# Attention outputs normalised through memory: stores, column reciprocals, a spread over rows and a GpSimd product in place of TensorE turns and VectorE divisions

## What is computed

```python
q = _split_heads(Q @ W_Q.T)
k = _split_heads(K @ W_K.T)
v = _split_heads(V @ W_V.T)
scores = jnp.einsum('bhqd,bhkd->bhqk', q, k) / jnp.sqrt(jnp.float32(DK))
scores = jnp.where(mask == 0, -jnp.inf, scores)
weights = jax.nn.softmax(scores, axis=-1)
attn = jnp.einsum('bhqk,bhkd->bhqd', weights, v)
attn = attn.transpose(0, 2, 1, 3).reshape(Q.shape[0], Q.shape[1], D)
return attn @ W_O.T
```

## Time and profile before

| | us |
|---|---|
| median of 3 runs | 1264.85 |
| lowest and highest run | 1264.16, 1265.81 |
| the profiled execution, device time | 1271.13 |
| span of its records | 1269.4 |
| PE busy | 1122.1 (88%) |
| DVE busy | 838.7 (66%) |
| ACT busy | 644.6 (51%) |
| POOL busy | 211.9 (17%) |
| granted PE clock, mean | 0.945 |

### The profile page before, as it was taken

How to read it: one execution, slowest core, us unless ns; L and a number is a source line. 1 busy time by engine, 2 the same in 40 slices (tenths; PEclk the granted TensorE clock), 3 DMA queues, 4 the chain that set the end, 5 groups by cost and what they waited for, 6 DMA issues and landing times. The chain is left out here.

```text
span 1269.4 us, 17696 instructions
## 1 busy us (share of the span) xinstructions
PE 1122.1 (88%) x5578; PEld 540.3 (43%) x5578; DVE 838.7 (66%) x2112; ACT 644.6 (51%) x1341; POOL 211.9 (17%) x273
## 2 busy tenths in 40 slices
PE   7889999999897999999859999996979999998480
PEld 4433343434453233333355666664523333335350
DVE  5788777776477899898752222224779888867622
ACT  3346666666543676767613333332427767674240
POOL 3310000000143000010212222212410010102244
PEclk9979999999999899999958999998979999999695
DMA  8943221220059334432471130102963323201054
GB/s 256 325 145 113 84 51 51 84 51 1 1 195 278 102 92 114 112 101 77 142 298 34 61 127 28 32 8 99 313 217 88 94 62 87 59 19 67 26 157 141
DMA packets 102868, 139.40 MB, mean 110 GB/s; under 512 B 11189, under 2 KB 84793, under 8 KB 101369
## 3 DMA queue, kind: packets, MB, share of 16 engines
q1 hardware_dynamic: 98696, 128.04, 33.2%
q0 software_dynamic: 4080, 10.23, 2.9%
HBM read 86.30 MB, written 52.17 MB: 109 GB/s over the span
## 5 line engine op out<-in xcount | busy, mean ns | idle before, releaser
L888 ACT ACTIVATE r<-ps 128x512 f32<-128x512 f32 x768 | 428.0, 600 | 209.5 <-PE ps L974 121.5
L377 DVE TENSOR_REDUCE m<-ps 128x1 f32<-128x512 f32 x512 | 320.6, 683 | 33.9 <-PE ps L961 33.9
L974 PE MATMUL ps<-r 99*128 99x512 bf16 x768 | 293.4, 387 | 6.4 <-ACT r L888 5.8
L961 PE MATMUL ps<-r 96*128 96x512 bf16 x720 | 282.2, 393 | 14.4 <-DVE m L377 7.0
L988 PE MATMUL ps<-r 128*32 128x512 f32 x1536 | 204.9, 605 | 5.6 <-ACT r L888 3.3
L373 DVE CUSTOM_DVE_ANT_0 r<-ps,r 128x512 bf16<-128x512 f32 x256 | 170.2, 690 | 53.2 <-PE ps L961 52.5
L974 PEld LDWEIGHTS ps<-r 99*128 99x128 bf16 x768 | 74.3, 98 | 213.8 <-ACT r L888 157.9
L961 PEld LDWEIGHTS ps<-r 96*128 96x128 bf16 x720 | 71.1, 99 | 103.1 <-DVE m L377 30.7
L864 POOL COPY r<-r 128x256 f32<-128x256 f32 x48 | 19.1, 401 | 524.5 <-PE ps L988 524.5
L978 PE MATMUL ps<-r,identb 128*128 128x512 bf16 x256 | 98.2, 384 | 0.0
L1661 DVE COPY r<-ps 128x512 f32<-128x512 f32 x46 | 31.8, 692 | 92.0 <-PE ps L1708 92.0
(11 more groups left out here) (152 smaller groups left out, 1197.7 us busy)
## 6 DMA issues: line engine op xcount, KB each, us to landing
r<-q_parts SPq DMA_DIRECT2D x48, 384.0 KB, 4.5
r<-k_parts SPq DMA_DIRECT2D x48, 384.0 KB, 5.4
k_parts<-r SPq DMA_DIRECT2D x24, 384.0 KB, 3.2
q_parts<-r SPq DMA_DIRECT2D x24, 384.0 KB, 3.2
r<-in_w SPq DMA_DIRECT2D x16, 512.0 KB, 3.7
r<-in_w SPq DMA_DIRECT2D x8, 1024.0 KB, 14.9
k_parts<-r SPq DMA_DIRECT2D x24, 256.0 KB, 3.2
q_parts<-r SPq DMA_DIRECT2D x24, 256.0 KB, 3.1
```

The lines of the kernel that those rows point to most:

```text
L377: ins = dve.tensor_reduce(out, mem.ps[:, bank, :], AX.X, ALU.max)
L888: act.activation(mem.probs[:, u // HG, u % HG, :], ps[:, ST + (UNITS * g + u) % DEEP, :], ACT.Exp, scale=SCALE).then_inc(a.p_exp.sem, 1)
L961: pe.matmul(ps[:, led_bank(n), :], mem.qst[g][0:ROWS, h, t * P:(t + 1) * P], mem.kst[g][0:ROWS, h, :], start=True, stop=True).then_inc(a.s ...
L974: ins = pe.matmul(out, mem.kst[g][0:KROWS, h, kt * P:(kt + 1) * P], mem.qst[g][0:KROWS, h, :], start=True, stop=not a.masked)
```

## The change

Groups 0 to 13 of each stage are no longer turned by PE and divided by DVE. ACT copies the products to `mem.ot` with a bias column (`guard`, 1e-30 on the four rows of sums, 0 elsewhere), and SP stores them to memory (`products`). Two groups are a chunk, 128 rows of outputs. SP loads a chunk's 8 rows of sums as 128 partitions of 32 columns (`sums`) and its outputs as 128x512 (`oTu`), once for every second group, at g = 2 for the batch's first chunk and at g = 0 of the next batch for its second. DVE takes the reciprocal of 128x32 at u = 12, SP stores it, and loads it back with every row repeated 16 times into `mem.oT`; POOL multiplies `oTu` by it in place. Groups 14 and 15 of a stage are turned and divided as before, and one `turn_out` is left at the stage's end. The tiles of the output projection move from (2, 3), (2, 4), (3, 3), (3, 4) to (2, 2), (2, 3), (2, 5), (2, 6). The store of the residual sum in sa0 stays at g = 3. The four shift semaphores become one. The diff, cut to its core:

```diff
...
+        self.sums = sb("sums", [P, C, S // DK])
+        self.recip = sb("recip", [P, C, S // DK])
+        self.guard = sb("guard", [P, 1])
...
         self.ot = take(self.r2, S, [S])
-        self.o = take(self.r2, T * D, [T, D])
+        self.oTu = take(self.r2, C * S, [C, S])
+        self.o = self.oTu[:, C - 1, :].rearrange("p (t d) -> p t d", t=T)
         self.oT = take(self.r2, C * S, [C, S])
...
 KEY_TILES = 2
 MASK_ROUNDS = T // KEY_TILES
 NEXT_STAGE = ((3, 5), (3, 14))
-HALF_TURN = (3, 13)
-LAST_TURN, LAST_OUT = (5, 2), (3, 4)
+LAST_TURN, LAST_OUT = 2, (3, 4)
+RECIP_STEP = 12
+TURNED = NG // C
+TURNED_FROM = B * NG - TURNED
 LATE = 2
 AHEAD = 3
 M_STEP, TURN_STEP = 8, 12
-OUT_TURNS = (3, 5)
-OUT_TILES = ((2, 3), (2, 4), (3, 3), (3, 4))
+OUT_TILES = ((2, 2), (2, 3), (2, 5), (2, 6))
...
+
+    def out_store(G):
+        sp.wait_ge(a.ot_sb.sem, a.ot_sb.at(G, 1))
+        sp.dma_start(a.dram["ot"][G], mem.ot).then_inc(a.sent.sem, 16)
+
+    def out_load(b, c):
+
+        G = NG * b + TURNED * c
+        sp.wait_ge(a.sent.sem, a.sent.at(G + TURNED))
+        if C * b + c:
+            sp.wait_ge(a.oT_sb.sem, C * b + c)
+        heads = a.dram["ot"][G:G + TURNED].rearrange("g (h r) n -> (g h) r n", h=HG)
+        sp.dma_start(mem.sums[:, c, :], heads[:, DK, :].rearrange("g (k n) -> g k n", k=DK))\
+          .then_inc(a.chunk_in.sem, 16)
+        sp.dma_start(mem.oTu[:, c, :], heads[:, 0:DK, :]).then_inc(a.chunk_in.sem, 16)
+
+    def recip_store(b, c):
+
+        sp.wait_ge(a.recip.sem, C * b + c + 1)
+        sp.dma_start(a.dram["recip"][b, c], mem.recip[:, c, :]).then_inc(a.recip_out.sem, 16)
+
+    def recip_spread(b, c):
+
+        sp.wait_ge(a.recip_out.sem, 16 * (C * b + c + 1))
+        if b:
+            sp.wait_ge(a.op_ps.sem, a.op_ps.at(b))
+        rows = a.dram["recip"][b, c].rearrange("(h k) n -> h (k n)", k=DK)
+        sp.dma_start(mem.oT[:, c, :], rows.unsqueeze(1).to_broadcast([P // DK, DK, S]))\
+          .then_inc(a.spread.sem, 16)
...
-            if a.self_block and g == OUT_TILES[-1][0] and not first:
+            if G >= 1 and G - 1 < TURNED_FROM:
+                out_store(G - 1)
+            chunk = (b, 0) if g == TURNED else (b - 1, 1) if g == 0 and not first else None
+            if chunk is not None:
+                out_load(*chunk)
+            if a.self_block and g == NG - 1 and not first:
                 store(b - 1)
             if not (last and g == NG - 1):
                 shift(*((b, g + 1) if g < NG - 1 else (b + 1, 0)))
             if a.masked and g == 0 and not last:
                 sp.wait_ge(a.mbS_ready.sem, a.mbS_ready.at(b, T))
                 load_mask(sp, a, b + 1)
+            if chunk is not None:
+                recip_store(*chunk)
             if meanwhile is not None:
                 meanwhile(sp, b, g)
+            if chunk is not None:
+                recip_spread(*chunk)
...
+    def divide(b, c):
+
+        pool.wait_ge(a.chunk_in.sem, a.chunk_in.at(C * b + c, 32))
+        pool.wait_ge(a.spread.sem, a.spread.at(C * b + c, 16))
+        pool.tensor_tensor(mem.oT[:, c, :], mem.oTu[:, c, :], mem.oT[:, c, :], ALU.mult).then_inc(a.oT_sb.sem, 1)
...
+    gather(0, 0)
+    gather(0, 1)
+    for b in range(B):
+        gather(b, 2)
+        if b:
+            divide(b - 1, 1)
+        gather(b, 3)
+        if b:
+            for k in range(2):
+                last_sums(pool, a, "pool", b - 1, k)
+        if b + 1 < B:
+            gather(b + 1, 0)
+        divide(b, 0)
+        if b + 1 < B:
+            gather(b + 1, 1)
...
     def out_copy(G):
         act.wait_ge(a.pv.sem, a.pv.at(G, T))
-        act.wait_ge(a.ot_ps.sem, a.ot_ps.at(G))
-        act.activation(mem.ot, ps[:, OB, :], ACT.Copy).then_inc(a.ot_sb.sem, 1)
-
-    def maxima(G, used=None):
+        if G <= TURNED_FROM:
+            act.wait_ge(a.sent.sem, a.sent.at(G))
+        else:
+            act.wait_ge(a.ot_ps.sem, G - TURNED_FROM)
+        act.activation(mem.ot, ps[:, OB, :], ACT.Identity, bias=mem.guard[:, 0:1]).then_inc(a.ot_sb.sem, 1)
...
-                if g == 1 and not first and u in OUT_TURNS:
-                    oT_copy(b - 1, OUT_TURNS.index(u))
                 if u == LATE and not (first and g == 0):
                     out_copy(G - 1)
...
-                    maxima(G + 1, (b, g))
-                if last and (g, u) == HALF_TURN:
-                    oT_copy(b, 0, LAST_TURN[0])
+                    maxima(G + 1)
...
         for t in range(T):
             ins = pe.transpose(ps[:, MISC, t * P:(t + 1) * P], mem.ot[:, t * P:(t + 1) * P], mem.ident[:, :])
         ins.then_inc(a.ot_ps.sem, 1)
-        misc[0] = (a.quotient.sem, a.quotient.at(G, QUOTIENT))
-
-    def turn_out(b, c, bank=MISC):
-        pe.wait_ge(a.quotient.sem, a.quotient.at(NG * b + (c + 1) * NG // C - 1, QUOTIENT))
-        if bank == MISC:
-            take_misc()
+        misc[0] = (a.quotient.sem, a.quotient.at(G - TURNED_FROM, QUOTIENT))
+
+    def turn_out(bank):
+        pe.wait_ge(a.quotient.sem, a.quotient.at(TURNED))
         for t in range(T):
-            ins = pe.transpose(ps[:, bank, t * P:(t + 1) * P], mem.o[:, t, c * P:(c + 1) * P], mem.ident[:, :])
+            ins = pe.transpose(ps[:, bank, t * P:(t + 1) * P], mem.o[:, t, :], mem.ident[:, :])
         ins.then_inc(a.oT_ps.sem, 1)
-        if bank == MISC:
-            misc[0] = (a.oT_sb.sem, a.oT_sb.at(b, c + 1))
...
-                if g == 1 and not first and u in OUT_TURNS:
-                    turn_out(b - 1, OUT_TURNS.index(u))
                 if u == M_STEP and not (last and g == NG - 1):
                     maxima(G + 1)
-                if u == TURN_STEP and not (first and g == 0):
+                if u == TURN_STEP and G > TURNED_FROM:
                     turn(G - 1)
                 if (g, u) in OUT_TILES and not first:
                     project_out(b - 1, OUT_TILES.index((g, u)))
-                if last and (g, u) == HALF_TURN:
-                    turn_out(b, 0, LAST_TURN[0])
...
-
+    def reciprocals(b, c):
+
+        dve.wait_ge(a.chunk_in.sem, a.chunk_in.at(C * b + c, 32))
+        dve.reciprocal(mem.recip[:, c, :], mem.sums[:, c, :]).then_inc(a.recip.sem, 1)
+
+    def normalise(G):
...
-                if u == TURN_STEP + 1 and not (first and g == 0):
-                    normalise(G - 1, b if g else b - 1, (g - 1) % NG, first)
+                if u == TURN_STEP + 1 and G > TURNED_FROM:
+                    normalise(G - 1)
+                if u == RECIP_STEP and g == TURNED:
+                    reciprocals(b, 0)
+                if u == RECIP_STEP and g == 0 and not first:
+                    reciprocals(b - 1, 1)
...
+        "ot": nc.dram_tensor("products", (B * NG, P, S), F32, kind="Internal").ap(),
+        "recip": nc.dram_tensor("reciprocals", (B, C, P, S // DK), F32, kind="Internal").ap(),
...
+            pool.memset(mem.guard[:, :], 0.0).then_inc(setup, 1)
+            for h in range(HG):
+                pool.wait_ge(setup, 15 + h)
+                pool.affine_select(out=mem.guard[:, :], in_=mem.guard[:, :], compare_op=ALU.not_equal, fill=1e-30,
+                                   base=-(h * VW + DK), pattern=[[0, 1]], channel_multiplier=1).then_inc(setup, 1)
...
```

More of the change, by code:

```diff
@@ L264, in __init__ @@
         self.stacks = [sig(f"stacks{s}", 32) for s in range(NG)]
-        self.shift = [sig(f"shift{s}", 16 * T) for s in range(NG)]
+        self.shift = sig("shift", 16 * T)
         self.s_ps = sig("s_ps", UNITS)
@@ L275, in __init__ @@
         self.ot_sb = sig("ot_sb", 1, 1)
-        self.ot_ps = sig("ot_ps", 1, 1)
+        self.sent = sig("sent", 16)
+        self.chunk_in = sig("chunk_in", 32)
+        self.recip = sig("recip", 1)
+        self.recip_out = sig("recip_out", 16)
+        self.spread = sig("spread", 16)
+        self.ot_ps = sig("ot_ps", 1)
         self.quotient = sig("quotient", QUOTIENT)
-        self.oT_ps = sig("oT_ps", C)
+        self.oT_ps = sig("oT_ps", 1)
         self.oT_sb = sig("oT_sb", C)
@@ L892, in out_copy, with maxima @@
         act.wait_ge(a.pv.sem, a.pv.at(G, T))
-        act.wait_ge(a.ot_ps.sem, a.ot_ps.at(G))
-        act.activation(mem.ot, ps[:, OB, :], ACT.Copy).then_inc(a.ot_sb.sem, 1)
-    def maxima(G, used=None):
+        if G <= TURNED_FROM:
[3 more added lines that the diff above has]
+        act.activation(mem.ot, ps[:, OB, :], ACT.Identity, bias=mem.guard[:, 0:1]).then_inc(a.ot_sb.sem, 1)
+    def maxima(G):
         act.wait_ge(a.m_ps.sem, a.m_ps.at(G, 1))
-        if used is not None:
-            b, g = used
-            act.wait_ge(a.shift[g].sem, a.shift[g].at(b, 16 * T))
+        if G:
+            act.wait_ge(a.shift.sem, a.shift.at(G))
         act.activation(mem.mT[:, :], ps[0:PARTS * T * HG, MISC, 0:P // 2].bitcast(BF16), ACT.Copy)\
@@ L908, in mask_copy, with oT_copy @@
                        ps[:, bank, :].bitcast(BF16), ACT.Copy).then_inc(a.mbT_ready.sem, 1)
-    def oT_copy(b, c, bank=MISC):
-        act.wait_ge(a.oT_ps.sem, a.oT_ps.at(b, c + 1))
```

(23 more changed lines are left out.)

11 lines of the change are left out of this document (5 added, 6 removed).

## The result

The changed kernel takes 1271.07 us (median of four runs, 1267.04 to 1272.74) against 1265.12 for the kernel before beside it: a ratio of 1.0041, 95% interval 1.0023 to 1.0059. A later series of twelve runs gave 1267.92 against 1265.52, 1.0011 (0.9996 to 1.0026). So the change costs between nothing and 0.4%; it was forecast to gain 0.2%.

What follows compares the result with a forecast made beforehand. PE's own work was taken to set the pace. Terms -26.1 + 15.1 + 2.3 + 1 + 2 gave -5.7, or -2.3 us with one clock fall (+3.4), hence 1262.6 us from the median 1264.85; range 1254 to 1272.

Steps and rivals of the forecast that it cites:

- What the change removes: On PE's path in all three stages: 42 turns, 18.5 us, and 21 turn-outs, 7.6 us, go; together 26.1 us gained.
- The bank: PE's third tile and maxima turn wait for the tiles' bank: +7.2 us in sa0, +3.9 xa1, +4 xa0; total +15.1.
- one fall of the clock: In sa0, PE's new waits bring one short fall to half clock, 6.8 us long, costing +3.4 us.
- the lost hiding: Two tiles no longer hide PE's wait of some 0.2 us for ACT's copy in a second group: +1 us.
- The rival of a fall in every batch: Clock falls in each of sa0's three batches: 1269.3 us with short falls, 1279.5 with long ones; chance 0.16.
- the rival without a fall: PE's clock does not fall, since products break up the waits: terms as priced, 1259.1 us; chance 0.27.
- The output copy: ACT's copy becomes an Identity with bias, +0.1 us in the 24 unmasked groups without tiles: +2.3 us.
- SP and the DMAs: SP's added stores and loads: shift 0.2 us late at no cost, little or no chunk wait in 8 places; +2, between 0 and 8.
- a wait on the shift and on the chunk: Sign of being wrong: a wait on the shift or chunk at units 0 and 12 in groups with g = 0; no size.
- The rival of late stores: SP waits for the store's landing, delaying chunk loads and shift; 3 us later than estimated gives 1281 us; chance 0.14.
- the rule weighed beside the term: A DMA pattern beginning with 8 heads uses 8 engines, doubling the 0.8 us size-dependent part; +2 would become about +5.

Runs made afterwards that it cites:

- tiles alone: The kernel before with only the four output tiles moved to the changed kernel's places (steps 2, 3, 5, 6 of one group): 1282.76 us, ratio 1.0146 to before.
- late tiles: The changed kernel with its last two output tiles moved from steps 5 and 6 to 12 and 13: 1254.78 us, 0.9919 to before; again 1253.21, 0.9902.

## Why the prediction was wrong

The time (1262.6) was 5 to 8.5 us low, and a gain was forecast where the first series shows a loss; the range held it. By the steps of the sum:

- **What the change removes, -26.1:** held, as far as the runs separate it. Groups without turns are 0.35 shorter with the copy's 0.09 in them, xa0 is 5.5 us shorter, and from tiles alone to the whole change it is 13 to 17 us, where this term less the copy's 2.3 and the exchange's 7 is 16.8.
- **The bank, +15.1, and one fall of the clock, +3.4:** held. 1.67 and 2.53 us were measured for 1.6 and 2.7, at the longest 1.0 and 0.2 for 1.2 and 0.1 without the block input. Tiles alone cost 18.5 us in the runs, where these terms and the lost hiding make 19.5. The clock fell twice, for 3.4 us each, at about 1.5 us each: by the earlier trace rows I had expected one fall of twice that length, so that the total came out right by luck. The rival of a fall in every batch had the number nearly right (two of three) and the price too high. Against the rival without a fall I had said that no wait between 0.56 and 2.75 had kept the clock. That was a misreading: in the same trace PE waited 1.75 us before 45.92, 1.54 before 372.74 and 385.89 and 1.59 before 396.96, at full clock each time.
- **The output copy, +2.3:** 0.09 us was measured for 0.1; its sum is within what the runs can tell. The +1 for the lost hiding was not measured by itself.
- **SP and the DMAs, +2 of 0 to 8: this is the step that failed.** It measured some 7 us (an estimate, by proportion from 15 of 21 chunks). The step took no cost for the shift, on 1.49 us between the end of its issues and the next group. But the shift has to land as well: in the trace of before its last semaphore event comes 1.06 us behind the issues, and so only 0.4 of the 1.49 was slack. In the group shown above the shift started 1.8 us late, not 0.2, and landed 1.35 behind its issues, and PE waited 1.65. The chunk loads took 1.34 to issue instead of 0.9, and the chunk landed 4.4 us after its issue (978.59 to 982.94) instead of 2.6; over all 21 the landing took 3.9 to 4.4, so DVE did wait, 9.5 us in all. For the products' landing, 6.5 was near the middle, but one number stood for a spread: in the twelve groups of sa0 and xa1 that load both operands and a chunk, they landed between 5.70 and 8.67 us in (7.65 in the one shown), and the three latest (7.65, 8.67 and 8.10) gave PE waits of 1.65, 1.64 and 0.94, most of the 5.1. The 6.5 was also not what its own figures add up to: the copy's end at 3.5 and the 4.6 of the earlier trace rows make 8.1. The prediction named a wait on the shift and on the chunk as signs that it was wrong, and both came. The rival of late stores, given 0.14, had this mechanism, and put the point from which the change loses at 1 us of lateness. It came about in its mildest form: not in every place, and 7 us, not 18.

On the chunk's landing the rule weighed beside the term was the better guide. The semaphore of the two chunk loads shows one event at each issue, then eight from 979.82 to 980.07, and eight from 982.51 to 982.94, while the store of 128 partitions shows sixteen spread over 975.74 to 977.88. The Trainium skill, DMA: Bandwidth & Descriptors, section "Why a DMA increments its semaphore by 16 and not by 1", says that only the engines in use report and the sequencer adds the rest at once: by that, a pattern that begins with 8 heads ran on 8 engines, and the trace agrees with its eight events. By the rule my term would have been +5. That the 8 engines are why the landing takes 4.1 us (median) is not shown: the quickest of the 42 stores of the same size landed in 2.0, but a store is not a load, and a pattern that begins with 16 rows was not tried.

So the sum with measured terms is -26.1 + 18.5 + 2.3 + 7 = +1.7 us, at the lower end of the +1.4 to +5.2 of the two ratios; what the first series has above it, up to 3.5 us, stays open. The mechanism was forecast, in the sum or in a rival. What failed was the size of the SP and DMA term: it counted the shift's landing as slack, and took a value near the bottom of a wide interval where lateness decided the sign.

## What to carry to other kernels

Work that is taken off the bounding engine is worth its time only if what it leaves does not crowd a shared buffer: here the same four tiles cost 18 us in one place and some 5 in another (an estimate: -26.1 + 2.3 + 7 is -16.8 without them, and late tiles gained 10.3 and 12.4), so move them before judging the idea. Before a wait for a DMA goes onto an in-order queue, add up what is ahead of that DMA in the queue and what is behind the wait; and check the last round of a stage by itself, since a later product there held up the next stage (5.25 us of DVE's wait at the end of sa0).

## What the hardware did that I had not expected

- TensorE's clock fell for 3.4 us only, behind waits of 2.5 us, and rose again while PE worked through; the shorter of the two in the earlier trace rows was 6.8 us. And the same wait need not give a fall: with only the tiles moved, PE's turn of the maxima waited 2.54 us in two batches, and the stretch behind it had full clock in one and half in the other, where it stayed for 6.8 us.

```profile
506.70:510.10 3.40, 3.40 (x22) 1.41 (x22) 2.32 (x5) 2.28 (x5) 1.74 (x2) 1.00 0.03 8
564.45:567.85 3.40, 3.40 (x13) 0.60 (x13) 1.05 (x2) 0.87 (x2) 1.71 (x2) 0.50 0.01 2
```

- The chunk loads and the spread took SP 0.59 to 0.70 us each to issue, one of them for 16 KB, against 0.34 for a store of 256 KB.
- A store of 16 KB landed after 1.4 us in a quiet queue, and held SP for 3.57 behind over 1 MB of loads and the products' store.
